# MetaFormer block with a top-2 mixture of experts: VectorE scales a tile's y inside the next tile, and always all three blocks

## What is computed

```python
t = _to_tokens(x)                       # 2048 tokens x 256
xt = _ln_t(t)
gate = softmax(xt @ Wg)                 # 8 experts, the two best kept, scaled to sum 1: scores
for e in range(8):
    h = gelu(xt @ W1[e] + b1[e])        # 256 -> 1024
    ye = h @ W2[e] + b2[e]              # 1024 -> 256
    out = out + ye * scores[:, e:e+1]
t = t + out
```

## Time and profile before

| | us |
|---|---|
| median of 3 runs | 426.71 |
| lowest, highest | 425.75, 428.63 |
| the profiled execution, its own time | 427.16 |
| its span in the trace | 425.4 |

### The profile page before, as it was taken

How to read it: one execution, slowest core, us unless ns; L and a number is a source line. 1 busy time by engine, 2 the same in 40 slices (tenths; PEclk the granted TensorE clock), 3 DMA queues, 4 the chain that set the end, 5 groups by cost and what they waited for, 6 DMA issues and landing times.

```text
span 425.4 us, 8138 instructions
## 1 busy us (share of the span) xinstructions
PE 372.0 (87%) x2476; PEld 333.7 (78%) x2477; DVE 264.9 (62%) x693; ACT 248.1 (58%) x522; POOL 177.6 (42%) x271
## 2 busy tenths in 40 slices
PE   6989969988998776999979999989999999989960
PEld 4535557877787755999969898989989998989960
DVE  5768477796898995465448344784447753834430
ACT  1577566647516861666538556785557855764530
POOL 5700000003045344326652564656646456656553
PEclk9999999999996555899999999999999999999995
DMA  8800000000020773619321932469323724233342
GB/s 278 257 12 2 0 1 2 0 2 1 2 99 2 300 257 89 230 18 258 60 49 22 258 54 51 84 204 255 55 51 64 223 43 72 39 51 54 49 58 30
DMA packets 22966, 38.63 MB, mean 91 GB/s; under 512 B 2576, under 2 KB 17296, under 8 KB 22800
## 3 DMA queue, kind: packets, MB, share of 16 engines
q0 software_dynamic: 8032, 12.82, 17.9%
q1 hardware_dynamic: 14896, 25.41, 17.2%
HBM read 28.85 MB, written 9.37 MB: 90 GB/s over the span
## 4 chain that ended last, share of the span: by engine, by line
PE 38%; POOL 10%; issue 8%; DVE 2%; DMA 1%; POOLq 1%; DVEq 1%; ACT 1%; ACTq 0%
POOL xg L521 8%; PE banks L1534 6%; PE banks L1233 6%; PE banks L1234 6%; PE banks L1235 6%; PE banks L1536 5%; PE banks L1538 5%; PE banks L1511 3%; DVE h_lo L1183 1%; DVE y_out L1207 1%; PE banks L1566 1%; DMA xg<-xn_rows,idx_in 1%; POOL idx_in L516 1%; POOL idx_out L559 1%; POOL out_rows L567 0%
## 5 line engine op out<-in xcount | busy, mean ns | idle before, releaser
L790 ACT ACTIVATE h_raw<-banks,b1t 128x256 f32<-128x256 f32 (+1 forms) x136 | 67.6, 497 | 86.3 <-PE banks L1235 85.6
L1183 DVE TENSOR_TENSOR h_lo<-h_raw,h_hi 128x256 fp32r<-128x256 f32 (+1 forms) x136 | 57.9, 441 | 64.5 <-ACT h_hi L793 62.8
L1534 PE MATMUL banks<-w_hi,h_hi 128*128 128x256 f32 x288 | 84.3, 293 | 9.3 <-DVE h_lo L1183 9.3
L1234 PE MATMUL banks<-x_lo,w_hi 128*128 128x256 f32 (+1 forms) x272 | 79.2, 291 | 3.2 <-issue 3.2
L1536 PE MATMUL banks<-w_lo,h_hi 128*128 128x256 f32 x288 | 81.4, 283 | 0.0
L1538 PE MATMUL banks<-w_hi,h_lo 128*128 128x256 f32 x288 | 81.4, 283 | 0.0
L1233 PE MATMUL banks<-x_hi,w_hi 128*128 128x256 f32 (+1 forms) x272 | 80.1, 295 | 0.8 <-issue 0.7
L1235 PE MATMUL banks<-x_hi,w_lo 128*128 128x256 f32 (+1 forms) x272 | 79.2, 291 | 0.0
L567 POOL DMA_INDIRECT out_rows<-y_out,idx_out x36 | 62.3, 1730 | 33.7 <-DVE y_out L1207 27.9
L521 POOL DMA_INDIRECT xg<-xn_rows,idx_in x57 | 57.8, 1014 | 27.9 <-POOL idx_in L516 16.3
L793 ACT ACTIVATE h_hi<-banks,b1t 128x256 fp32r<-128x256 f32 (+1 forms) x136 | 67.3, 495 | 0.0
(11 more groups left out here) (219 smaller groups left out, 680.7 us busy)
## 6 DMA issues: line engine op xcount, KB each, us to landing
w_raw<-in_w SPq DMA_DIRECT2D x16, 1024.0 KB, 7.9
xn_rows<-xn SPq DMA_DIRECT2D x2, 1056.0 KB, 5.0
x<-in_x_tok SPq DMA_DIRECT2D x4, 512.0 KB, 5.8
out_rows<-x SPq DMA_DIRECT2D x1, 2048.0 KB, 9.3
b2b<-in_b SPq DMA_DIRECT2D x1, 1024.0 KB, 4.6
xg<-xn_rows,idx_in POOLq DMA_INDIRECT x57
out_rows<-y_out,idx_out POOLq DMA_INDIRECT x36, 4.0
out_rows<-x POOLq DMA_DIRECT2D x1, 384.0 KB, 3.2
```

Of the source, the lines that this page charges most:

```text
L790: act.activation(h_raw[j % RING][:, 0:w], banks[:, j % RING, 0:w], ACT.Gelu, bias=bias)
L1183: dve.tensor_tensor(h_lo[:, j, 0:w], h_raw[j % RING][:, 0:w], h_hi[:, j, 0:w].bitcast(F32), ALU.subtract).then_inc(h_split, 1)
L1234: pe.matmul(out, a_hi, b_lo, start=False, stop=False)
L1534: pe.matmul(out, h_hi[:, j, r], w_hi[e % 2][:, c], start=j == 0 and i < 2, stop=False, skip_group_check=width == WIDE)
```

## The change

VectorE's scaling of tile t moves from the end of tile t into tile t + 1, behind the first h_lo there. It waits there for the same three semaphores. It always treats three blocks. In a 2-wide tile the third holds what lay in y_sum before, and GpSimd still adds only the blocks that the tile has. A memset gives the third block of y_sum a value ahead of the first tile, and the last tile's scaling comes after the loops. The other engines' programs are the same.

```diff
+            def y_scaled(t, e):
+
+                dve.wait_ge(y_free, t + 1)
+                dve.wait_ge(scores_moved, t + 1)
+                dve.wait_ge(y_taken, t + 2)
+                for i in range(WIDE):
+                    ins = dve.tensor_scalar(y_out[:, i, :], y_sum[:, i, :], score[:, i, e:e + 1], None, ALU.mult)
+                ins.then_inc(y_weighted, 1)
+
+            def tile(t, e, width, split, prior):
+
                 w = width * P
                 for j in range(HJ):
                     dve.wait_ge(gelu_done, t * HJ + (j + 1 + RING))
                     dve.wait_ge(l2_done, t * HJ + (j + 1))
                     dve.tensor_tensor(h_lo[:, j, 0:w], h_raw[j % RING][:, 0:w], h_hi[:, j, 0:w].bitcast(F32),
                                       ALU.subtract).then_inc(h_split, 1)
+                    if j == 0 and prior is not None:
+                        y_scaled(t - 1, prior)
                     if split and e + 1 < E:
...
                 ins.then_inc(y_taken, 1)
 
-                dve.wait_ge(y_free, t + 1)
-                dve.wait_ge(scores_moved, t + 1)
-                dve.wait_ge(y_taken, t + 2)
-                for i in range(width):
-                    ins = dve.tensor_scalar(y_out[:, i, :], y_sum[:, i, :], score[:, i, e:e + 1], None, ALU.mult)
-                ins.then_inc(y_weighted, 1)
-
-
+
+
+            dve.memset(y_sum[:, 2, :], 0.0).then_inc(dve_step, 1)
+            steps[0] += 1
+            dve.wait_ge(dve_step, steps[0])
             dve.sem_inc(h_split, RING)
...
+                prior = e - 1 if e else None
                 with dve.If(odd):
-                    tile(t0, e, WIDE, True)
+                    tile(t0, e, WIDE, True, prior)
                 with dve.Else():
-                    tile(t0, e, 2, True)
+                    tile(t0, e, 2, True, prior)
                 with dve.If(more):
                     with dve.Fori(t0 + 1, t1) as t:
-                        tile(t, e, 2, False)
+                        tile(t, e, 2, False, e)
                 t0 = t1
+            y_scaled(t0 - 1, E - 1)
```

More of the change, by code:

```diff
@@ L1176, in x_low @@
                                   ALU.subtract).then_inc(x_split, 1)
-            def tile(t, e, width, split):
+            def y_scaled(t, e):
[6 more added lines that the diff above has]
+            def tile(t, e, width, split, prior):
                 w = width * P
```

## The result

The changed kernel takes 420.7 us (median of 6 runs, 418.62 to 422.75) against 425.44 of the kernel before in its 6 runs: a ratio of 0.9872, with a 95% interval of 0.9834 to 0.991. A second series gave 420.15 and 0.989 (0.9862 to 0.9918). So the kernel is some 5 us faster, where 9.1 were forecast, and the time lies in the range. The kernel before stood at 426.71 in the 3 runs that the forecast started from and at 425.44 in these 6. The move does what it was said to do, but a third to a half of its gain is lost on the way.

A forecast was written before the change was run, and what follows sets the result against it. TensorE was taken as the bound, its weight loads waiting 11.9 us for h_lo behind y_free. Gross gain 11.4 less 0.6 (late h_lo), 1.4 (gathers) and 0.3 (end) gave 9.1: 417.7 us from 426.71, range 414 to 422.5.

The forecast's parts named there:

- The spare time of h_lo in the ordinary tile: First h_lo of an ordinary tile: done at 249.45, wanted by TensorE at 250.09, so 0.6 us to spare.
- GpSimd's 0.75 us of slack: GpSimd in an ordinary tile: needs 11.5 us of TensorE's 12.25, so 0.75 us per tile are left.
- GpSimd costs nothing: GpSimd over a whole tile: it keeps up despite the third block, so it adds 0 to the time.
- a rival in which both take 2.12 us in every tile: Rival 2: GpSimd becomes the bound, both adds taking 2.12 instead of 1.58 us; 432.9 us, chance 0.04.
- the 0.67 us hole behind y_out: VectorE leaving one program piece for the next: moved between y_sum and h_lo, where it waits for ScalarE anyway.
- Late h_lo at the second step: TensorE's second step of layer 2: h_lo now behind y_out comes late, 0.6 us in all, bounds 0 and 2.
- The gathers: Turns in t4, t7, t8: tokens land too late for the faster TensorE; 1.4 us given back, bounds 0 and 3.5.
- The end (0.3): Behind the last tile: the third block's scaling is on the path and adds 0.3 us.
- The third block: VectorE's y_out: 0.26 us more in each of 15 tiles, 3.9 in all, hidden until the end.
- rival 3: Three tiles with weights on the way: gathers give back 3.5 instead of 1.4 us; 419.8 us, chance 0.12.
- rival 4: Start of t3: the unexplained 3.19 us stall goes (414.5 us) or comes twice (420.9); chance 0.06 both ways together.
- Rival 1: Second h_lo late in every tile, the wait for y_free replacing the old stall: 424.2 us, chance 0.10.

The follow-up runs named there:

- e4: The changed kernel with four one-element memsets, each waited for, behind y_out in first tiles: 418.20 us, 0.9817 of the kernel before.
- e5: The changed kernel with three memsets of 128 elements a partition, not waited for, behind y_out in first tiles: 418.82 us, 0.9864 of the kernel before.
- e14: As e1, with the three memsets of e5 between y_out and the first h_lo in first tiles: 422.98 us, 0.994 of the kernel before.
- e9: As e6, with ScalarE's w_hi also one step later and the third block scaled at the end of 3-wide tiles: 418.05 us, 0.9848 of the kernel before.
- e3: The changed kernel scaling two blocks always, with zeros in the third block of y_out: 417.88 us, 0.981 of the kernel before.
- e6: The changed kernel with w_lo of each step behind h_lo of the next step in first tiles: 419.43 us, 0.9875 of the kernel before.
- e12: As e9, with SyncE issuing an expert's weights only behind the gather under way in the same first tile: 413.44 us, 0.9715 of the kernel before.
- e1: The changed kernel with scaling ahead of the first h_lo in experts' first tiles, behind it only in inner tiles: 426.52 us, 1.001 of the kernel before.

## Why the prediction was right, and where it was short

The main mechanism was right. The first h_lo stood behind y_free, and out of that order TensorE no longer waits for it. The spare time of h_lo in the ordinary tile (0.57 us, from its end at 250.75 to TensorE's 251.32), GpSimd's 0.75 us of slack (0.94 less the 0.2 to 0.3 that it never loses), and the ordinary distance held to 0.1 us. Going by the distance from turn to turn, t5, t6, t9, t10, t15 and t16 gained 0.7 to 1.1 us each, within 0.13 of my terms.

The sum was 9.1 and came to some 5; in the stretch 6.1 instead of 9.0. By tiles 3.6 us are missing, against 0.7 more than forecast elsewhere. They are missing in first tiles and behind them: 0.99 in t14, 0.81 in t11, 0.75 in t7, 0.49 in t4, 0.33 in t8, 0.23 in t13.

- "GpSimd costs nothing" failed as a step. I reckoned its slack from an ordinary tile and allowed for longer adds only in a rival in which both take 2.12 us in every tile. The rival was right in kind and wrong in place: in first tiles alone, and with 4.4 instead of 2.1 us. What I overlooked stood in the earlier trace rows: the 0.67 us hole behind y_out. I booked its move as free, as VectorE waits for ScalarE there. Going by e4, e5 and e14 it was also what let GpSimd's add in: with a run of w_lo and h_lo directly behind y_out the first add of t7 takes 2.20 to 5.69 us, with memsets between them 1.64 to 1.96. The Trainium skill, "SBUF — State Buffer", section "Who interferes with whom", states that a VectorE instruction with two SBUF inputs contends with a GpSimd instruction that reads SBUF. The long adds agree with that; the second adds of e5, 1.85 us beside the same instructions, and the 1.73 us of t11 don't follow from it. The same section of the Trainium skill infers that `tensor_tensor` does not hold up the making of descriptors for GpSimd's DMAs. For the indirect DMA here the measurement decides otherwise: 4.41 us against 1.64.
- Late h_lo at the second step was put at 0.6 us in all, with 2 as its upper bound, and measured 2.6. t2 and t7, at 0.25 each, measured 0.21 and 0.30. t8, t13 and t14, where I had 0, 0.1 and 0, measured 1.17, 0.37 and 0.54; GpSimd's delay is handed on there.
- The start of a tile behind a first tile was not in the sum. TensorE's weight loads stand 0.91, 0.75 and 0.50 us there. e9 shows that it is ScalarE's order. That TensorE's stall for h_lo had given ScalarE the time to finish w_hi and x_hi is argued from this, not shown.
- The gathers were put at 0.5 in t4 and 0.8 in t8. t4 measured 1.0. t8 measured 0, for its tile was late anyway, and 1.5 to 2.0 as soon as something else was mended (e3, e5, e6, e9; 0.73 in e4). That it comes from the weights' loads is shown by e12, where they are issued 4 to 5 us later and the waits are gone.
- The end (0.3) was not measured by itself. The third block in all: e3 leaves the stretch as it is, though new waits for the gather may hide what it saves.
- The sentence "the forecast alone reaches from 415 to 420" doesn't follow from its terms: 417.7 with the two lower and the two upper bounds gives 415.7 and 421.2. And the 4.8 us from the turn to y_free are counted from idx_in at 244.76; the turn in t4 began at 243.59. Nothing hangs on this one.

That 420.7 lies in the range is partly luck. The range was widened for rival 3 (gathers) and rival 4 (the stall of t3), and what used it up was neither, but GpSimd's long adds, the late second h_lo and ScalarE's order. Rival 1 occurs, but in five tiles (t2, t7, t8, t13, t14) and not in all. The 3.19 us stall of the earlier trace rows stayed in every profile (2.4 to 3.3 us); its cause is open.

## What to carry to other kernels

When a wait is moved, also ask what its idle time was good for: here a hole of 0.67 us on VectorE went, and GpSimd's DMA was kept out; TensorE's stall went, and ScalarE's order began to cost. Reckon the slack of each engine in the fullest tile and not in the ordinary one. A chain through four engines gives back what one edit gains until the next limit is moved too. The changed order alone gave 1.1 to 1.3%; with w_lo and w_hi one step later and the third block scaled apart (e9) it was 1.5%, and with the loads issued 4 to 5 us later besides (e12) 2.9%.

## What the runs showed of the hardware

An indirect DMA that GpSimd starts took 1.63 to 1.64 us in first tiles when three memsets of VectorE stood ahead of w_lo (e5), and up to 5.69 us when `tensor_tensor` instructions with both inputs in SBUF followed y_out without a break (e1). It doesn't take turns with them. The profiles of the changed kernel and its variants have 34 adds of more than 2.15 us; 33 end 1.50 to 1.52 us behind the end of a VectorE instruction and one 1.45 behind it. In 28 of them it is the first place behind y_out where the next row overlaps by less than the usual 0.07 to 0.09 us. The first hole that one can see is there, or 0.6 to 1.1 us later (0.67 in t7 of the changed kernel).

A gather on GpSimd's queue kept TensorE waiting up to 2.01 us when 2 MB of weights had been issued some 4 us behind the turn (e9), and not at all when they were issued 4 to 5 us later (e12).
